# Where the streamed matmul operands start within 512 bytes of the on-chip memory

## The chip, the cores and the metric

The kernel runs on one core of a Trainium2 chip. The metric is device time in microseconds (us) of that core, from one execution of the whole program. Before the change it is 384.46 us, the median of 3 runs (384.4 to 384.72).

## The reference, cut to what matters

The input `x` has 8 sequences of 512 tokens with 128 features. Three blocks follow one another, each on a layer-normalised `x`, each added to `x`:

```
h = silu(x @ w1.T * s1) * (x @ w2.T * s2)     # 128 -> 512 (layers "0" and "1" of the code)
h = gelu(h @ h1.T * s)                        # 512 -> 512
h = gelu(h @ h2.T * s)                        # 512 -> 512
y = h @ w3.T * s3                             # 512 -> 128
x = x + 0.5 * y                               # then a recurrence, then the same again
```

The middle block is a recurrence over the 512 tokens, `h = tanh(x_t B + h A^T)` with 16 states, whose states go through `C` and `W_out`. All arrays are float32. The weights `w1`, `w2`, `h1`, `h2`, `w3` hold only -1, 0 and 1, so one fast matmul form is exact in them, while the activations need two parts.

## The kernel before, in words

Features lie on the 128 partitions, tokens along the free dimension. The tokens are cut into 8 chunks of N = 512; the feed-forward block runs 16 times (`g` from 0 to 15: 8 chunks before the recurrence, 8 after it). Every product of a feed-forward layer is made by `split_mm` (line 270): for each 128x128 tile of weights there are two TensorE matmuls of 512 columns, one that streams the high part of the activations and one that streams the low part, both into the same PSUM bank. The operand that streams past the array (the moving one) is a slice of 2,048 bytes in each partition; the other is loaded beforehand by a weight load (LDWEIGHTS) of 128 columns, 512 bytes in each partition. The rows write a matmul's inputs as moving, loaded: `y_hi,w_hi`.

The high parts are written as float32r (`xn_hi` by ScalarE at line 1190, `y1_hi` by ScalarE or VectorE, `y2_hi` and `y3_hi` by ScalarE at line 1216); the low parts are differences that VectorE (lines 802, 837) and GpSimd (lines 1489, 1495) write. In the text, layer 1 is the pair `w1`, `w2`, which streams `xn_hi` and `xn_lo`; layer 2 streams `y1_hi`, `y1_lo`; layer 3 `y2_hi`, `y2_lo`; layer 4 `y3_hi`, `y3_lo`.

The order of the work is written out by hand for each engine. A turn of TensorE (`early_turn`, `middle_turn`, `turn`) runs layer 2 of chunk `g`, layer 4 of `g - 1` within it, then layer 1 of `g + 1` between pieces of layer 3 of `g`. Between groups of 4 to 16 such streams stand short matmuls: transposes (4 of 128 columns at a time, line 282, 292 or 302, which stream `ident`), single steps of the recurrence (32 columns, line 437, which stream `h` against `a_mix`), and the products with `b_rep` and `cw_mix`. Engines wait for each other by semaphores; none of these waits depends on addresses.

What matters here is where tiles lie. `sb()` (line 61) reserves them one behind the other in the order of the calls. The small tiles and `gap` (line 105) end at byte 18,432 of each partition, which is 36 times 512. From there every tile is a multiple of 512 bytes: `w_raw`, `w_hi`, `w_lo`, and behind them all activations. So each weight tile that is loaded and each slice that is streamed begins at a multiple of 512 bytes. `WOFF` (line 72) and the sizes of the tiles make this so.

Of the kernel before, what the change touches and what calls it, by code (L numbers as in the profile page):

```python
# [21 lines left out]
F32R = mybir.dt.float32r  # L22
# [5 lines left out]
P = 128  # L28
# [12 lines left out]
N = HALVES * HCOLS  # L41
# [17 lines left out]
def build(nc, xT, xtok, w1T, w2T, h1T, h2T, w3T, scales, Ablk, Brep, CTrep, WoutT, ident_d, mask_d, outT):  # L59
    with ExitStack() as ctx:  # L60
        def sb(name, shape, dt=F32):
            return ctx.enter_context(nc.sbuf_tensor(name, shape, dt))
# [51 lines left out]
        outb = sb("outb", [P, N])  # L114
        xnt_f = sb("xnt_f", [P, N])
        xnt_m = sb("xnt_m", [P, N])
        xn_hi = sb("xn_hi", [P, N], F32R)
        xn_lo = sb("xn_lo", [P, N], F32R)
        xn2 = sb("xn2", [P, N])
        xb_all = sb("xb_all", [P, CHUNKS * HCOLS])  # L120
        th = sb("th", [P, 2, N])
        u = sb("u", [P, 2, N])
        y1 = sb("y1", [P, KT, N])
        y23 = sb("y23", [P, KT, N])
        y1_hi = sb("y1_hi", [P, KT, N], F32R)
        y1_lo = sb("y1_lo", [P, KT, N], F32R)
        y2_hi = sb("y2_hi", [P, KT, N], F32R)
        y2_lo = sb("y2_lo", [P, KT, N], F32R)
        y3_hi = sb("y3_hi", [P, KT, N], F32R)
        y3_lo = sb("y3_lo", [P, KT, N], F32R)  # L130
        ident = sb("ident", [P, P])
# [1550 lines left out]
```

## Time and profile before

| | us |
|---|---|
| median of 3 runs | 384.46 |
| the profiled execution | 385.06 |
| its span, first to last instruction | 383.1 |
| TensorE busy | 376.4 (98%) |
| VectorE busy | 279.7 (73%) |
| ScalarE busy | 268.0 (70%) |
| GpSimd busy | 163.9 (43%) |

The span is what the trace covers; 2.0 us of the profiled execution lie around it. A busy time says how long the engine had something in hand. For TensorE that says little of its pace, since matmuls overlap: the next one starts while the last one drains. The pace is read from the distance between the starts of two matmuls. Weight loads have their own rows (PEld) and lie beside the matmuls. "ns of one" is the time that the trace gives to one instruction, its drain included.

### The profile page before, as it was taken

Reading aid. Unit: us, or ns where it says so; the run is one execution under the profiler, and the core shown is the slowest. Engines: PE = TensorE matmul, PEld = TensorE weight load, DVE = VectorE, ACT = ScalarE, POOL = GpSimd, SP = SyncE. Lnnn points to the kernel's source line nnn. Section 1 sums busy time; section 2 is a strip of 40 time slices with the busy share of each in tenths; the row PEclk is TensorE's granted clock in tenths of the full one; section 3 lists DMA queues with packets and bytes.
Section 4 is the critical chain, followed back from the end, with each engine's and each line's share of the span. In section 5 each row is a group of like instructions: output and inputs, shape, how many; then the busy total and the mean of one; then the engine's idle time right before and its main releaser. Section 6 shows DMA issues by size and latency. Waiting matters only on the chain.

```text
span 383.1 us, 6587 instructions
## 1 busy us (share of the span) xinstructions
PE 376.4 (98%) x1793; PEld 300.2 (78%) x1793; DVE 279.7 (73%) x724; ACT 268.0 (70%) x625; POOL 163.9 (43%) x156
## 2 busy tenths in 40 slices
PE   8999999999999999999999999999999999999995
PEld 6777777778878787878778788888888888887774
DVE  4878989896777677576868866776767677686713
ACT  3889595777858688576784767758576775757654
POOL 3555262655525355142551633525334352533421
PEclk9999999999999999999999999999999999999999
DMA  7920000000000000000001001010100101000001
GB/s 226 436 110 1 27 2 27 3 2 28 2 28 0 2 27 0 28 2 28 27 2 56 2 8 49 0 55 2 41 14 0 55 0 55 0 30 26 2 28 32
DMA packets 6365, 14.00 MB, mean 37 GB/s; under 512 B 1088, under 2 KB 2112, under 8 KB 6080
## 3 DMA queue, kind: packets, MB, share of 16 engines
q1 hardware_dynamic: 5328, 13.37, 9.1%
q10 hardware_dynamic: 1008, 0.29, 0.3%
q8 instruction: 12, 0.20, 0.2%
q14 instruction: 17, 0.14, 0.1%
HBM read 7.37 MB, written 2.10 MB: 25 GB/s over the span
## 4 chain that ended last, share of the span: by engine, by line
PE 85%; issue 7%; POOL 3%; ACT 3%; DVE 2%; POOLq 0%; DVEq 0%
PE F L274 66%; PE FR L274 7%; PE SC L491 2%; PE FR L302 2%; POOL y_lo L1489 1%; PE SC L422 1%; POOL y_lo L1495 1%; PE F L519 1%; ACT y_hi L1216 1%; PE FR L292 1%; PE SC L274 1%; PE MI L302 1%; ACT y L1213 1%; PE F L521 1%; PE MI L282 1%
## 5 line engine op out<-in xcount | busy, mean ns | idle before, releaser
L274 PE MATMUL F<-y_hi,w_hi 128*128 128x512 f32 (+1 forms) x484 | 196.6, 407 | 0.3 <-DVE y_lo L1045 0.2
L274 PE MATMUL F<-y_lo,w_hi 128*128 128x512 f32 (+1 forms) x484 | 188.6, 390 | 0.0
L274 PEld LDWEIGHTS F<-y_hi,w_hi 128*128 128x128 f32 x484 | 90.9, 188 | 20.7 <-issue 2.2
L1213 ACT ACTIVATE y<-F,sc 128x512 f32<-128x512 f32 x111 | 76.1, 686 | 41.3 <-PE F L274 40.1
L274 PEld LDWEIGHTS F<-y_lo,w_hi 128*128 128x128 f32 x484 | 91.2, 188 | 15.9
L837 DVE TENSOR_TENSOR y_lo<-y,y_hi 128x512 fp32r<-128x512 f32 x79 | 64.8, 821 | 39.2 <-ACT y_hi L1216 39.2
L1489 POOL TENSOR_TENSOR y_lo<-y,y_hi 128x512 fp32r<-128x512 f32 x48 | 66.7, 1398 | 59.1 <-DVE y_hi L824 48.5
L1495 POOL TENSOR_TENSOR y_lo<-y,y_hi 128x512 fp32r<-128x512 f32 x48 | 62.6, 1310 | 34.6 <-ACT y_hi L1216 34.4
L1216 ACT ACTIVATE y_hi<-F,sc 128x512 fp32r<-128x512 f32 x111 | 76.1, 685 | 0.0
L1232 ACT ACTIVATE h<-SC 128x32 fp32r<-128x32 f32 x96 | 18.8, 196 | 48.0 <-PE SC L437 46.8
L274 PE MATMUL F<-xn_hi,w_hi 128*128 128x512 f32 x118 | 49.5, 419 | 0.1
L807 DVE SCALAR_TENSOR_TENSOR u<-th,F 128x512 f32<-128x512 f32 x61 | 41.5, 681 | 7.0 <-ACT th L1195 7.0
L274 PE MATMUL F<-xn_lo,w_hi 128*128 128x512 f32 x118 | 46.3, 393 | 0.0
L1481 POOL TENSOR_TENSOR ve_f<-mv_f,epsc 128x4 f32<-128x4 f32 x16 | 3.2, 202 | 96.6 <-DVE mv_f L768 91.6
L817 DVE SCALAR_TENSOR_TENSOR y<-F,s12h,u 128x512 f32<-128x512 f32 x58 | 43.3, 747 | 1.6
L1195 ACT ACTIVATE th<-F,s1h 128x512 f32<-128x512 f32 x61 | 41.1, 689 | 3.2 <-PE F L274 2.4
L856 DVE TENSOR_TENSOR h<-SC,h 64x32 fp32r<-64x32 f32 x96 | 17.1, 178 | 19.0 <-ACT SC L1233 18.2
L274 PEld LDWEIGHTS F<-xn_hi,w_hi 128*128 128x128 f32 x118 | 22.1, 187 | 6.9 <-DVE y L817 1.3
L274 PEld LDWEIGHTS F<-xn_lo,w_hi 128*128 128x128 f32 x118 | 22.2, 189 | 3.4
L274 PE MATMUL FR<-y_hi,w_hi 128*128 128x512 f32 x60 | 24.0, 399 | 0.0
L274 PE MATMUL FR<-y_lo,w_hi 128*128 128x512 f32 x60 | 23.4, 390 | 0.0
L437 PEld LDWEIGHTS SC<-h,a_mix 128*128 128x128 f32 x95 | 17.8, 188 | 6.6 <-DVE h L856 2.9
(170 smaller groups left out, 439.6 us busy)
## 6 DMA issues: line engine op xcount, KB each, us to landing
x_all<-in_xT SPq DMA_DIRECT2D x1, 2048.0 KB, 16.1
x_all<-x1c SPq DMA_DIRECT2D x8, 256.0 KB, 2.3
x_all<-lnin SPq DMA_DIRECT2D x8, 256.0 KB, 2.2
out<-outb SPq DMA_DIRECT2D x7, 256.0 KB, 2.0
x_all<-in_xtok SPq DMA_DIRECT2D x1, 1536.0 KB, 12.0
w_raw<-in_h1T SPq DMA_DIRECT2D x2, 512.0 KB, 7.8
w_raw<-in_h2T SPq DMA_DIRECT2D x2, 512.0 KB, 9.3
x_all<-in_xtok SPq DMA_DIRECT2D x2, 128.0 KB, 3.2
```

The lines of the kernel that those rows point to most:

```text
L274: mm = nc.tensor.matmul(out, wtile(w, layer, k, m), y, start=first and i == 0, stop=last and i == len(pairs) - 1)
L437: nc.tensor.matmul(SC[:, span(t)], a_mix[:, :], states, start=False, stop=True, skip_group_check=True).then_inc(step_mm, 1)
L807: nc.vector.scalar_tensor_tensor(out=u[:, m % 2, :], in0=th[:, m % 2, :], scalar=1.0, in1=l1_banks(g, m, late)[0][:, :], op0=ALU.add, op1= ...
L817: nc.vector.scalar_tensor_tensor(out=y1[:, m, :], in0=l1_banks(g, m, late)[1][:, :], scalar=s12h[:, m:m + 1], in1=u[:, m % 2, :], op0=ALU. ...
L837: nc.vector.tensor_tensor(y_lo[:, k, :], y[:, k, :], y_hi[:, k, :].bitcast(F32), ALU.subtract).then_inc(out_sem, 1)
L856: nc.vector.tensor_tensor(h[0:64, span(t)], SC[0:64, span(CSTEPS + t)], h[0:64, span(t)].bitcast(F32), ALU.subtract).then_inc(step_h, 1)
L1195: nc.scalar.activation(th[:, m % 2, :], l1_banks(g, m, late)[0][:, :], ACT.Tanh, scale=s1h[:, m:m + 1]).then_inc(th_r, 1)
L1213: nc.scalar.activation(y23[:, m, :], bankt[:, :], ACT.Gelu, scale=s)
L1216: nc.scalar.activation(y_hi[:, m, :], bankt[:, :], ACT.Gelu, scale=s).then_inc(hi_r, 1)
L1232: nc.scalar.activation(h[:, span(t)], SC[:, span(t)], ACT.Tanh)
L1489: pool.tensor_tensor(y1_lo[:, m, :], y1[:, m, :], y1_hi[:, m, :].bitcast(F32), ALU.subtract).then_inc(y1_lo_r if m < KT - 1 else y1_lo_las ...
L1495: pool.tensor_tensor(y_lo[:, k, :], y[:, k, :], y_hi[:, k, :].bitcast(F32), ALU.subtract).then_inc(out_sem, 1)
```

## The change

Four pads are added, and `xn_hi` and `xn_lo` are reserved later. Nothing reads or writes the pads. No instruction, order, semaphore or loop is changed; only addresses are.

```diff
-        xn_hi = sb("xn_hi", [P, N], F32R)
-        xn_lo = sb("xn_lo", [P, N], F32R)
         xn2 = sb("xn2", [P, N])
         xb_all = sb("xb_all", [P, CHUNKS * HCOLS])
         th = sb("th", [P, 2, N])
         u = sb("u", [P, 2, N])
         y1 = sb("y1", [P, KT, N])
         y23 = sb("y23", [P, KT, N])
+        past_x = sb("past_x", [P, 64])
+        xn_hi = sb("xn_hi", [P, N], F32R)
+        xn_lo = sb("xn_lo", [P, N], F32R)
+        past_1 = sb("past_1", [P, 80])
         y1_hi = sb("y1_hi", [P, KT, N], F32R)
         y1_lo = sb("y1_lo", [P, KT, N], F32R)
+        past_2 = sb("past_2", [P, 16])
         y2_hi = sb("y2_hi", [P, KT, N], F32R)
         y2_lo = sb("y2_lo", [P, KT, N], F32R)
+        past_3 = sb("past_3", [P, 80])
         y3_hi = sb("y3_hi", [P, KT, N], F32R)
         y3_lo = sb("y3_lo", [P, KT, N], F32R)
         ident = sb("ident", [P, P])
```

A pad of 64 floats is 256 bytes, one of 80 is 320, one of 16 is 64. Summed up and taken within 512, the streamed parts then begin 256 bytes (layer 1), 64 (layer 2), 128 (layer 3) and 448 (layer 4) past a multiple of 512. The weights stay where they were. `xn2`, `xb_all`, `th`, `u`, `y1` and `y23` lie 4,096 bytes lower and still at multiples of 512. The tiles behind the last pad (`ident`, `a_raw`, `a_mix`, `ct`, `wout`, `cw_rep`, `cw_mix`, the parts, `h`) lie 960 bytes higher, so 448 past a multiple of 512.

## Rows read from the trace of the kernel before

**Rows 1.** The page's busy times, and its line of the granted clock.
```profile
PE 376.4 (98%) x1793; PEld 300.2 (78%) x1793; DVE 279.7 (73%) x724; ACT 268.0 (70%) x625; POOL 163.9 (43%) x156
...
PEclk9999999999999999999999999999999999999999
```
**Rows 2.** Busy times by stretch: engines, then granted clock, DMA share, GB/s.
```profile
60.00:175.00 115.00, 114.92 (x580) 91.49 (x578) 86.28 (x242) 85.17 (x216) 52.60 (x51) 1.00 0.03 12
175.00:220.00 45.00, 45.00 (x230) 35.04 (x228) 36.39 (x102) 29.92 (x73) 18.56 (x19) 1.00 0.06 24
220.00:350.00 130.00, 130.00 (x614) 105.98 (x614) 93.43 (x234) 90.43 (x229) 53.86 (x47) 1.00 0.06 25
```
**Rows 3.** The chain that ended last, by engine.
```profile
PE 85%; issue 7%; POOL 3%; ACT 3%; DVE 2%; POOLq 0%; DVEq 0%
```
**Rows 4.** TensorE's groups by form: count, busy us, mean ns of one.
```profile
L274 PE MATMUL F<-y_hi,w_hi 128*128 128x512 f32 x476 | 194.4, 408 | 0.1
L274 PE MATMUL F<-y_lo,w_hi 128*128 128x512 f32 x476 | 186.6, 392 | 0.0
L274 PE MATMUL F<-xn_hi,w_hi 128*128 128x512 f32 x118 | 49.5, 419 | 0.1
L274 PE MATMUL F<-xn_lo,w_hi 128*128 128x512 f32 x118 | 46.3, 393 | 0.0
L274 PE MATMUL FR<-y_hi,w_hi 128*128 128x512 f32 x60 | 24.0, 399 | 0.0
L274 PE MATMUL FR<-y_lo,w_hi 128*128 128x512 f32 x60 | 23.4, 390 | 0.0
L302 PE MATMUL FR<-ident,xnt_f 128*128 128x128 f32 x60 | 9.6, 283 | 0.0
...
L274 PE MATMUL F<-xn_lo,w_lo 128*128 128x512 f32 x3 | 1.2, 389 | 0.0
```
**Rows 5.** Matmuls in order of time, late in a run of streams: start, duration.
```profile
127.16 0.39 PE L274 MATMUL F<-y_lo,w_hi 128*128 128x512 f32 x1
...
128.52 0.39 PE L274 MATMUL F<-y_lo,w_hi 128*128 128x512 f32 x1
```
**Rows 6.** Matmuls in order of time, behind four transposes.
```profile
180.56 0.60 PE L292 MATMUL FR<-ident,lnin 128*128 128x128 f32 x4
180.91 0.48 PE L274 MATMUL F<-y_hi,w_hi 128*128 128x512 f32 x1
181.22 0.40 PE L274 MATMUL F<-y_lo,w_hi 128*128 128x512 f32 x1
...
181.69 0.40 PE L274 MATMUL F<-y_lo,w_hi 128*128 128x512 f32 x1
181.93 0.39 PE L274 MATMUL F<-y_hi,w_hi 128*128 128x512 f32 x1
182.15 0.39 PE L274 MATMUL F<-y_lo,w_hi 128*128 128x512 f32 x1
...
183.08 0.40 PE L274 MATMUL F<-y_lo,w_hi 128*128 128x512 f32 x1
```
**Rows 7.** Weight loads in the stretch of Rows 5, then their group by form.
```profile
127.17 0.19 PEld L274 LDWEIGHTS F<-y_hi,w_hi 128*128 128x128 f32 x1
...
L274 PEld LDWEIGHTS F<-y_lo,w_hi 128*128 128x128 f32 x484 | 91.2, 188 | 15.9
```
**Rows 8.** A stream with no weight load beside it, all engines.
```profile
215.02 0.40 PE L274 MATMUL F<-y_lo,w_hi 128*128 128x512 f32 x1
215.35 0.16 PEld L422 LDWEIGHTS SC<-xn,b_rep 128*32 128x32 f32 x8 [0.37 <-ACT xn L1228]
```
**Rows 9.** The page's groups that write low parts, with idle time before.
```profile
L837 DVE TENSOR_TENSOR y_lo<-y,y_hi 128x512 fp32r<-128x512 f32 x79 | 64.8, 821 | 39.2 <-ACT y_hi L1216 39.2
L1489 POOL TENSOR_TENSOR y_lo<-y,y_hi 128x512 fp32r<-128x512 f32 x48 | 66.7, 1398 | 59.1 <-DVE y_hi L824 48.5
L1495 POOL TENSOR_TENSOR y_lo<-y,y_hi 128x512 fp32r<-128x512 f32 x48 | 62.6, 1310 | 34.6 <-ACT y_hi L1216 34.4
```

## The prediction

> **What bounds the kernel now.** I read the busy times first. TensorE has something in hand for 98% of the span, and the granted clock is full in every slice, which is its level of 2.4 GHz [rows 1]. By stretch the picture is sharper: from 60 to 350 us TensorE is busy 289.92 of 290 us, while VectorE has 216.1 and ScalarE 205.5 [rows 2]. The chain that ended last lies on TensorE for 85% and on issue for 7% [rows 3]. So time is set by how closely TensorE's matmuls follow one another, and not by how long another engine takes.
>
> Most of them are streams of 512 columns. The six groups of high and low parts in [rows 4] hold 2 x (476 + 118 + 60) = 1,308. Their busy times overlap, so I take the pace from starts. Late in a run of streams, six intervals take 128.52 - 127.16 = 1.36 us, or 226.7 ns each [rows 5]. I call this the settled pace; a stream there is given 0.39 us. Behind four transposes it is another: the first stream takes 181.22 - 180.91 = 0.31 us to the next, and the eight intervals after it take 183.08 - 181.22 = 1.86 us, or 232.5 ns each, single ones lasting 0.22 and 0.24 [rows 6]. The instruction is the same, its width is the same, no engine is waited for. At 2.4 GHz, 512 columns alone take 213.3 ns. So there are two losses: 13.4 ns in each settled stream, and another 6 ns or so in the unsettled ones.
>
> What differs between the two stretches? Not the weight tile: both walk through tiles that lie 512 bytes and more apart, and all streams begin at multiples of 512. Bits of the address above 512 therefore do not look like the cause. What is left is the phase in which one read falls against another, and the start within 512 bytes, which is the same everywhere in this trace. The next weight load starts within 0.01 us of its stream (127.17 against 127.16) and takes 188 ns of the 227 [rows 5, 7]. Two reads of the same memory then run side by side, one of 2,048 bytes and one of 512, both from the start of a 512-byte block. That is the one thing the change touches.
>
> **The change part by part.** *Instructions.* It adds and removes none: no DMA, no wait, no semaphore. A pad costs nothing at run time. What follows is all about the duration of instructions that stay.
>
> *The streams.* The trace has no stream at another offset, so I bound the effect from rows. The groups of low parts are the clean ones, because they never stand behind a short matmul. Their means are 392, 393 and 390 ns [rows 4] against 389 for a settled stream (the 0.39 of [rows 5], to the nanosecond in the small group at 389 of [rows 4]). The excess is 476 x 3 + 118 x 4 + 60 x 1 = 1,960 ns, 2.0 us. The high parts run in the same stretches, alternating with them, so they carry the same 2.0 us, besides the 0.09 us (0.48 against 0.39, [rows 6]) that each first one behind a short matmul loses because its successor's weights can only then be loaded. That last loss is one of order, and I leave it. If the shift lets the two reads fall in without colliding, all streams run at the settled pace: 4.0 us less. By the same measure the mean pace now is 226.7 + 3 = 229.7 ns.
>
> Beyond that the settled pace itself may move, since it is 13.4 ns above the 213.3 of the array. Bounds by rows: at the shortest single interval, 0.22 us, the streams would give 1,308 x 9.7 ns = 12.7 us; at 213.3 ns, 1,308 x 16.4 = 21.5 us. On the other side, at the unsettled 232.5 ns throughout they would cost 1,308 x 2.8 = 3.7 us; at the longest single interval, 0.24 us, 13.5 us, which no stretch of the trace holds for long. I take the 4.0 us, and 1.5 us for the settled pace (an estimate: about a tenth of its 13.4 ns, 1.2 ns on 1,308 streams). A whole removal is not likely, because a stream with no weight load beside it (the next load only 0.33 us after its start) is still given 0.40 us and not less [rows 8]; ends of matmuls are modelled, so this speaks only softly. Sum: -5.5 us.
>
> *The short matmuls.* `ident`, `a_mix`, `cw_mix` and `h` move by 448 within 512. Four transposes and their hand-over take 180.91 - 180.56 = 0.35 us [rows 6]. Were each transpose to change by 3 ns as the streams do, the 60 of the largest group [rows 4] would move 0.2 us, with either sign. The steps of the recurrence are 32 columns each, a sixteenth of a stream. I take nothing for both.
>
> *The other engines.* VectorE and GpSimd write the low parts to shifted places, at 821, 1,398 and 1,310 ns of one, and both groups sit idle before it for 39.2, 59.1 and 34.6 us in all [rows 9]. With starts still at multiples of 64 bytes I take nothing. Their cover is that idle time: an extra 1% on GpSimd's 129 us is 1.3 us and is swallowed by it. Where that cover is thin, in the 3% of the chain that lies on GpSimd [rows 3], 1% would cost 0.1 us. If TensorE becomes quicker by 5.5 us over 16 chunks, that is 0.34 us per chunk; VectorE, with 216 us of work in 290, does not become the bound [rows 2], but single waits on it and on ScalarE will eat some tenths of a microsecond, which I count into the range.
>
> **From span to time.** The profiled execution took 385.06 us with a span of 383.1. Less 5.5 it is 379.6. The median of the runs lies 0.6 lower than the profiled one, so I forecast 379.0 us.
>
> **The rivals.**
>
> *It changes nothing.* If the two reads have ports of their own, the start within 512 bytes can't matter and the unsettled pace has its cause within TensorE, for instance in how weights and streams are handed over. For it: the soft sign of [rows 8], where a stream alone isn't shorter, and that transposes, whose operands begin at multiples of 512 as well, run without a visible loss. Against it: the pace wanders between 0.22 and 0.24 us with nothing else to make it do so [rows 6]. It gives 384.5 us. The Trainium skill states this rule: "SBUF — State Buffer", section "Who interferes with whom", gives TensorE two independent read ports, one for the moving operand and one for weight loads, and says that it never waits on anyone. By that rule the change would be worth zero. The same skill's "TensorE: Matmul & The Clock Gate", section "Back-to-back issue gap", gives N/2.4 + 2.5 ns, an estimate of 215.8 ns for 512 columns; the trace does not agree, it has 226.7 at best over a run. So something costs these streams more than the pages tell, and that is why I give their rule less than half.
>
> *It is slower.* The order of short matmuls and streams stays, and with it the times at which runs of streams begin. With other offsets a run may never fall into the settled pace: then the streams of [rows 5] behave like those of [rows 6]. Place: every run longer than ten streams, above all layer 2 and 3. Price: 232.5 instead of 229.7 ns on 1,308 streams, +3.7 us, 388.2 us. It decides as soon as the mean pace exceeds 229.7. For it: the mean pace now, 229.7, lies midway between the settled 226.7 and the unsettled 232.5, so the pace that a random phase gives is about the present mean or worse. Against it: settling is what the streams do by themselves when left alone, so a phase without collisions exists and draws them in; it would be odd if only the offset 0 had one.
>
> *It is much faster.* The 13.4 ns of the settled pace are a collision too, of two reads that begin on the same 512-byte boundary at the same time, and the shift takes them away. At 1 to 2 ns above the array, about 215 ns, the streams save 1,308 x 14.7 = 19.2 us and the time is 365.3. For it: the loss is in every stream, as the equal starts are. Against it: [rows 8].
>
> **How the numbers follow.** Chances: forecast (the pace falls to between 220 and 229 ns, 372 to 383.6 us) 0.56; nothing 0.18; slower 0.18; much faster 0.08. The likeliest case alone has a range of 374 to 382.5. For 8 in 10 I leave out the much faster case and the worse half of the slower one, and put the ends at 370 (just past the 0.22 us bound, which is 371.8) and 387.5. About 0.2% (0.8 us) is what a measurement of this kernel can tell from no change. The forecast and the much faster case make faster 0.64, nothing makes the same 0.17 (a small part of it falls to each side), slower is 0.19.
>
> **What would show it.** In the profile of the changed kernel: TensorE's counts stay 1,793 and 1,793. The mean of the low-part groups falls from 392 and 393 to 389 or less, the starts behind transposes lie 227 ns apart at once and not after ten streams; if the settled pace moves, 128.52 - 127.16 has its like with less than 1.36 us. Layers 1 to 4 have different offsets, so if offsets matter they should show different paces, while the first stream behind a short matmul keeps its 0.31 us. Wrong would be: low-part groups at 392 again (nothing), or at 394 and more (slower). If they fall and the time doesn't, waits on VectorE, ScalarE or GpSimd have taken the gain, and the idle time before TensorE's weight loads would have grown. If the time falls while the starts keep their distances, the gain is from the writers of the low parts, which I have put at nothing.

## The result and the profile after

The changed kernel takes 386.85 us (median of 4 runs, 386.15 to 386.94) against 384.46. The ratio is 1.0062, 95% interval 1.0047 to 1.0077: slower by 2.4 us, where 5.5 us less had been forecast.

The page of the changed kernel, the lines that answer to [rows 1] (engine, busy us, instructions; then the clock by slice):

```profile
span 384.9 us, 6587 instructions
...
PE 378.0 (98%) x1793; PEld 299.5 (78%) x1793; DVE 279.9 (73%) x724; ACT 267.8 (70%) x625; POOL 164.1 (43%) x156
...
PEclk9999999999999999999999999999999999999999
```

Same instructions, same clock, and VectorE, ScalarE and GpSimd as busy as before. TensorE's groups by form, answering to [rows 4]:

```profile
L278 PE MATMUL F<-y_hi,w_hi 128*128 128x512 f32 x476 | 195.3, 410 | 0.1
L278 PE MATMUL F<-y_lo,w_hi 128*128 128x512 f32 x476 | 187.5, 394 | 0.0
L278 PE MATMUL F<-xn_hi,w_hi 128*128 128x512 f32 x118 | 49.5, 419 | 0.1
L278 PE MATMUL F<-xn_lo,w_hi 128*128 128x512 f32 x118 | 46.4, 393 | 0.0
L278 PE MATMUL FR<-y_hi,w_hi 128*128 128x512 f32 x60 | 24.2, 403 | 0.0
L278 PE MATMUL FR<-y_lo,w_hi 128*128 128x512 f32 x60 | 23.6, 394 | 0.0
```

Layer 1 (`xn`) stays at 393. The group into bank FR, which is layer 3's second row of tiles, goes from 390 to 394, the large mixed group from 392 to 394. The stretch of [rows 5], the same eight streams of layer 3, in the changed kernel (start, duration):

```profile
127.10 0.39 PE L278 MATMUL F<-y_lo,w_hi 128*128 128x512 f32 x1
127.34 0.39 PE L278 MATMUL F<-y_hi,w_hi 128*128 128x512 f32 x1
...
128.50 0.39 PE L278 MATMUL F<-y_lo,w_hi 128*128 128x512 f32 x1
```

Six intervals now take 1.40 us, 233.3 ns each, where they took 226.7. And the stretch of [rows 6], layer 2 behind four transposes:

```profile
180.77 0.60 PE L296 MATMUL FR<-ident,lnin 128*128 128x128 f32 x4
181.12 0.48 PE L278 MATMUL F<-y_hi,w_hi 128*128 128x512 f32 x1
181.44 0.40 PE L278 MATMUL F<-y_lo,w_hi 128*128 128x512 f32 x1
...
183.28 0.40 PE L278 MATMUL F<-y_lo,w_hi 128*128 128x512 f32 x1
```

Its eight intervals take 1.84 us, 230 ns each, against 232.5. So the change did act on the unsettled streams, and it took the settled pace away.

To sum this up I matched every matmul with its place in the program. For each stream I took the distance from its start to the start of the matmul behind it, left out those of 245 ns and more, and averaged them by layer, from layer 2 of chunk 1 to the start of the last chunk's layer 3:

| streams of (their number before) | offset | before, ns | after, ns |
|---|---|---|---|
| layer 1 (189) | 256 | 230.0 | 231.2 |
| layer 2 (425) | 64 | 230.2 | 231.0 |
| layer 3 (393) | 128 | 229.3 | 232.6 |
| layer 4 (117) | 448 | 229.4 | 232.9 |

Together these are 1,124 distances of 229.8 ns on average before (258.25 us) and 1,123 of 231.8 ns after (260.27 us). 2.0 ns on each of 1,124 is 2.3 us. From the start of chunk 2 (its first layer 1 stream) to the start of the last chunk's layer 3 TensorE needs 320.26 us before and 322.23 after, +1.97: the distances left out, and the short matmuls, took a little less. The profiled spans differ by 1.8 us only, because the changed kernel reached chunk 2 0.5 us earlier. Its warm-up streams were over sooner. The first row is before, the second after:

```profile
1.47 7.48 PE L491 MATMUL SC<-y_lo 128*128 128x512 f32 x19 [1.47 <-DVE y_lo L1060]
1.47 5.93 PE L495 MATMUL SC<-y_lo 128*128 128x512 f32 x19 [1.47 <-DVE y_lo L1064]
```

In the kernel before, 13 of the distances within these 19 are 426 or 427 ns, which is 512 columns at the clock's lower level of 1.2 GHz; after, 5 are. In the nine kernels of the experiments below it is 5 to 12, with the warm-up's two tiles always at the same start, so this is when the clock rose in an execution and not the addresses.

### The profile page after: what moved, and what is told of

Read it like the earlier page. It is cut to its first block, busy times and chain, and to the rows that moved or that the text cites. A ratio compares the mean times of both kernels' runs of the same rounds, so it can differ in the third digit from the quotient of the medians.

```text
span 384.9 us, 6587 instructions
## 1 busy us (share of the span) xinstructions
PE 378.0 (98%) x1793; PEld 299.5 (78%) x1793; DVE 279.9 (73%) x724; ACT 267.8 (70%) x625; POOL 164.1 (43%) x156
## 4 chain that ended last, share of the span: by engine, by line
PE 83%; issue 7%; POOL 4%; ACT 3%; DVE 1%; DMA 1%; SPq 0%; POOLq 0%; DVEq 0%
PE F L278 66%; PE FR L278 7%; PE FR L306 2%; POOL y_lo L1493 1%; DMA w_raw<-in_w2T 1%; PE F L523 1%; PE SC L426 1%; POOL y_lo L1499 1%; PE FR L296 1%; ACT y_hi L1220 1%; PE SC L278 1%; ACT y L1217 1%; PE MI L306 1%; PE F L525 1%; PE MI L286 1%
## 5 line engine op out<-in xcount | busy, mean ns | idle before, releaser
L1493 POOL TENSOR_TENSOR y_lo<-y,y_hi 128x512 fp32r<-128x512 f32 x48 | 66.8, 1395 | 59.8 <-DVE y_hi L828 48.5
L1499 POOL TENSOR_TENSOR y_lo<-y,y_hi 128x512 fp32r<-128x512 f32 x48 | 62.9, 1315 | 34.8 <-ACT y_hi L1220 34.6
```

The source lines that it names most:

```text
L1493: pool.tensor_tensor(y1_lo[:, m, :], y1[:, m, :], y1_hi[:, m, :].bitcast(F32), ALU.subtract).then_inc(y1_lo_r if m < KT - 1 else y1_lo_las ...
L1499: pool.tensor_tensor(y_lo[:, k, :], y[:, k, :], y_hi[:, k, :].bitcast(F32), ALU.subtract).then_inc(out_sem, 1)
```

## The experiments

Three theories at the start. A: the *distance* between the start of the stream and the start of the loaded tile, taken within some power of two, sets the pace a run of streams settles to, and 0 happens to be good. B: the stream's own start decides. C: neither; the writers of the shifted tiles disturb TensorE.

### The pace by itself: sweep

A program with nothing but streams: 32 of them per case, both operands at chosen starts.

```diff
+        for (name, _, wat), s in zip(CASES, streamed):        # 21 cases
+            w = weights[wat]
+            matmul(banks[3][:, 0:32], w[:, 0:P], s[:, 0:32])  # one short matmul ahead of each run
+            for i in range(32):
+                matmul(bank, w[:, i // 2 % 4 * P:][:, 0:P], s[:, i % 2 * N:][:, 0:N])
```

> A program of its own that leaves the whole reference computation out: 32 streams of 512 columns (float32r, all zeros) for each start of the streamed tile, 0 to 480 bytes past a multiple of 512 in steps of 32, the loaded tile at 0; then both tiles moved alike (64, 128, 448), then the loaded tile alone at 128 and 448. Theory A (the distance between the two starts within 512 bytes sets the pace that a run settles to): offset 0 settles to 226.7 ns, 64 near 229, 128 near 232 to 233, 448 above 229, 256 near 227; both moved alike gives 226.7 each time; the loaded tile alone at 448 gives what the stream at 64 gives. Theory B (the stream's own start decides, whatever the load does): both moved by 64, 128, 448 repeat the paces of the streams at 64, 128, 448, and moving the loaded tile alone gives 226.7. Theory C (start has no part, the slower paces of the changed kernel come from the writers of the tiles, since here no engine writes while TensorE runs): 226.7 for every case.

Rows of the sweep, one short matmul and its run of 32 streams per case (`zero` is stream and load at 0; the `s_` names say the stream's start; `both_` moves load and stream alike; `w_` moves the load alone):

```profile
34.49 0.18 PE L68 MATMUL B<-zero,weights 128*128 128x32 f32 x1
34.52 7.55 PE L72 MATMUL B<-zero,weights 128*128 128x512 f32 x32
...
49.51 7.58 PE L72 MATMUL B<-s_sixtyfour,weights 128*128 128x512 f32 x32
...
64.54 7.68 PE L72 MATMUL B<-s_onetwoeight,weights 128*128 128x512 f32 x32
...
72.08 7.74 PE L72 MATMUL B<-s_onesixty,weights 128*128 128x512 f32 x32
...
94.83 7.51 PE L72 MATMUL B<-s_twofivesix,weights 128*128 128x512 f32 x32
...
139.97 7.71 PE L72 MATMUL B<-s_fourfoureight,weights 128*128 128x512 f32 x32
...
155.12 7.51 PE L72 MATMUL B<-both_sixtyfour,weights 128*128 128x512 f32 x32
...
177.31 7.68 PE L72 MATMUL B<-w_onetwoeight,weights 128*128 128x512 f32 x32
184.86 7.57 PE L72 MATMUL B<-w_fourfoureight,weights 128*128 128x512 f32 x32
```

The settled pace, as the mean of the 16th to the 30th start-to-start distance of each run. Where a run repeats in a cycle that doesn't divide 15, another 15 give up to 0.7 ns more or less:

| stream past load, bytes | 0, 256 | 32, 288 | 64, 320 | 96, 352 | 128, 384 | 160, 416 | 192, 448 | 224, 480 |
|---|---|---|---|---|---|---|---|---|
| ns | 226.67 | 233.5 | 228.9 | 233.3 | 232.4 | 234.3 | 233.3 | 233.2 |

Each pair of distances that differ by 256 bytes agrees within 0.1 ns. Both moved alike by 64, 128 and 448: 226.67 each time. The load alone at 128 (distance 384): 232.3; at 448 (distance 64): 228.9. No other engine writes in this stretch, so C falls as the cause of this; B falls with the `both_` cases. Here the distance within 256 bytes decides. A settled run isn't always even: at 0 its distances repeat as 226, 227, 227; at 128 as 228, 230, 233, 241, 232, 231, 232; each distance has a cycle of its own, and these cycles are there in the changed kernel's layers 2, 3 and 4.

### Both operands moved in the kernel

```diff
-        gap = sb("gap", [P, 136])
+        gap = sb("gap", [P, 152])
```
with the four pads of the change left out, so that weights, streams and all else behind `gap` start 64 bytes past a multiple of 512.

> Weights and streamed parts both start 64 bytes past a multiple of 512 (the pad ahead of the weights is 64 bytes longer, the four pads of the change are gone, xn_hi and xn_lo keep their later place). Theory A (distance decides): paces of before, 226.7 settled, 384.5 us within 0.3. Theory B (the stream's own start decides): all layers settle to 229 and wander near 231, about +1.5 us, 386 us.

384.44 us against 384.25, ratio 1.0000, interval 0.9987 to 1.0013. Its layer 2 takes 230.05 ns, and chunk 2 to the last layer 3 is 0.07 us shorter than before. So the absolute start, moved by 64 bytes, has no part in the kernel either, nor has the later place of `xn_hi` and `xn_lo`. This run also says what a mean by layer is worth: its layer 1 takes 230.6 ns (before: 230.0) and its layer 4 228.8 (229.4) with every distance as before. Differences of 0.6 ns in layers 1 and 4, which have the fewest streams, carry no meaning; layers 2 and 3 differ by 0.1.

### One layer at a time

```diff
-        past_1 = sb("past_1", [P, 80])
+        past_1 = sb("past_1", [P, 16])        # layer 2 alone: past_x, past_2 left out,
+        past_2 = sb("past_2", [P, 112])       # the next pad closes the 512 again
```
and likewise for each of the others.

> Only layer 1's streamed parts start 256 bytes past a multiple of 512. The sweep has the paces repeat every 256 bytes, so 256 is 0. Theory A (distance within 256 bytes): paces as before, 384.3 us within 0.3. Theory of a period of 512 bytes (256 is the far end): layer 1 slower by 2 to 6 ns on its 256 streams, +0.5 to +1.5 us.

> Only layer 2's streamed parts start 64 bytes past a multiple of 512. Theory A or B: its streams take about 231 ns against 230.15 before, +0.2 to +0.6 us. Theory C: no difference from before.

> Only layer 3's streamed parts start 128 bytes past a multiple of 512; layers 1, 2, 4 and all tiles behind them at multiples. In the changed kernel layer 3's streams took 232.6 ns on average against 229.3 before. Theory A or B (start sets the pace): layer 3 near 232.5, the other layers as before but for the phase they are entered with, +1.0 to +1.6 us, most of the change's +2.4. Theory C (writers or the new order of the tiles): all layers alike, and the time moves with none of the layers in particular.

> Only layer 4's streamed parts start 448 bytes past a multiple of 512, which settled at 233.3 ns in the sweep. Theory A: its 128 streams take about 233 ns against 229.4, +0.4 to +0.5 us, and the layer 2 streams behind them start unsettled, +0.1. If the four layers' costs add up (about 0 + 0.7 + 1.0 + 0.5 us), no other part of the change is needed for its +2.4.

| alone | ratio, 95% interval | its streams, ns | chunk 2 to last layer 3, us |
|---|---|---|---|
| layer 1 at 256 | 0.9999, 0.9989 to 1.0009 | 230.0 to 230.1 | +0.02 |
| layer 2 at 64 | 1.0018, 1.0007 to 1.0030 | 230.2 to 230.6 | +0.64 |
| layer 3 at 128 | 1.0022, 1.0010 to 1.0033 | 229.3 to 232.3 | +0.91 |
| layer 4 at 448 | 1.0022, 1.0008 to 1.0036 | 229.4 to 232.8 | +0.58 |

The four ratios sum to +0.61%, the change is +0.62%; each of them has an interval of about 0.1% to either side, so their sum is known to some 0.25%. The stretch gives the same picture: +2.15 us in sum against +1.97, and the two kernels whose distances are as before within 256 bytes (layer 1 alone, both operands moved) lie within 0.1 us of the kernel before. In the kernel with layer 3 alone the group into FR, which holds only layer 3, goes from 390 to 394, while layer 1's doesn't rise (the same form as in [rows 4]); with layer 2 or layer 4 alone FR stays at 391:

```profile
L276 PE MATMUL F<-xn_lo,w_hi 128*128 128x512 f32 x118 | 46.3, 392 | 0.0
...
L276 PE MATMUL FR<-y_lo,w_hi 128*128 128x512 f32 x60 | 23.6, 394 | 0.0
```

Layer 1 at 256 costs nothing, as a period of 256 bytes says. The 1.2 ns that layer 1 lost in the changed kernel then come from something else, likely from its neighbours: with layer 4 alone moved it takes 230.8. Layer 2 costs more than its own streams do: of its 0.64 us only 0.2 are its own (425 x 0.46 ns); in its run layer 4 goes from 229.4 to 231.2, another 0.2 us, which is well above what traces differ by. Layer 3 rises by 0.4 ns; the 0.5 ns of layer 1 are within what traces differ by. My reading, which no run shows by itself, is that a run that is at another point of its cycle hands that on to the next layer.

### A uniform bad distance

```diff
-        past_x = sb("past_x", [P, 64])
+        past_x = sb("past_x", [P, 40])
-        past_1 = sb("past_1", [P, 80])
-        past_2 = sb("past_2", [P, 16])
-        past_3 = sb("past_3", [P, 80])
+        past_4 = sb("past_4", [P, 88])
```

> The streamed parts of all four layers start 160 bytes past a multiple of 512, the distance whose settled pace was the slowest of the multiples of 32 in the sweep, 234.3 ns; the tiles behind them at multiples of 512. Theory (the settled pace of the distance sets the time): the mean pace goes from 229.7 to about 234.3 ns, and 1,250 streams that follow a stream give +5.7 us, 1.5% slower, near 390 us. If the time depends only on how often runs enter unsettled, or on layers being at different offsets from each other, it stays near 384.5 to 386.

387.86 us, ratio 1.0099, interval 1.0084 to 1.0115. The mean pace came out at 233.9 ns, near the 234.3 of the sweep, and 4.1 ns more on 1,124 streams are 4.6 us. But chunk 2 to the last layer 3 grows by 3.4 us only. One stream before had waited, with 473 ns to the next start; that wait is gone (336 ns). The short matmuls take 0.6 us less, 0.4 of it at the steps of the recurrence, and there the idle time of TensorE's weight loads that VectorE's `h` ended goes from 2.9 to 2.5 us, that ended by its `y` from 1.3 to 0.9. So the mechanism was as expected, and of my +5.7 us, 1.1 were too high a pace and too many streams; the rest is in part that a slower TensorE waits less for VectorE. The three groups of low parts:

```profile
L276 PE MATMUL F<-y_lo,w_hi 128*128 128x512 f32 x476 | 188.4, 396 | 0.0
L276 PE MATMUL F<-xn_lo,w_hi 128*128 128x512 f32 x118 | 46.6, 395 | 0.0
...
L276 PE MATMUL FR<-y_lo,w_hi 128*128 128x512 f32 x60 | 23.7, 395 | 0.0
```

### Is anything better than 0, and what is the floor?

The second sweep takes finer starts, narrower loads, shorter streams, and bfloat16. Its loop is the first one's, with the number of loaded and streamed columns and the type as further parameters of a case.

> The reference computation is left out. 32 streams per case again, the loaded tile at 0. (1) Streams at 4, 8, 12, 16, 24, 40, 48, 80, 240 and 252 bytes. Theory A, distance within 256 bytes counted in lines of 16 bytes or so: 4 to 12 repeat 0 (226.7 ns), 16 and 240 are new values between 226 and 235; if one is under 226.7, a faster kernel follows. Theory A', distance counted in 64-byte blocks: 4 to 24 lie between the 226.7 of 0 and the 233.5 of 32, growing with distance. (2) Loads of 96, 64 and 32 columns beside the same streams at 0, and of 64 and 32 at 128. If the losses are two reads that meet, the loss falls with the length of the load: 226.7 falls towards 216 at 32 columns, and the 232.4 at 128 falls more. If the 13.4 ns over 213.3 is a fixed cost of a float32r stream, 226.7 stays for every load at 0. (3) Streams of 384 columns (160 ns at full clock): meeting reads leave the same 13 ns and 19 ns as with 512; a cost per column leaves 10 and 14. (4) bfloat16 for both operands, half the bytes: meeting reads need less of the memory, about 216 at every start; a fixed phase effect would show the same spread between 0, 32 and 128.

```profile
39.01 7.81 PE L76 MATMUL B<-s_four,weights 128*128 128x512 f32 x32
...
54.21 7.61 PE L76 MATMUL B<-s_twelve,weights 128*128 128x512 f32 x32
...
129.46 7.57 PE L76 MATMUL B<-loads_thirtytwo,weights 128*32 128x512 f32 x32
...
151.72 5.79 PE L76 MATMUL B<-short_zero,weights 128*128 128x384 f32 x32
157.38 5.88 PE L76 MATMUL B<-short_onetwoeight,weights 128*128 128x384 f32 x32
...
177.00 7.07 PE L76 MATMUL B<-half_onetwoeight,weights_half 128*128 128x512 bf16 x32
```

Settled paces in ns: 4 bytes 236.7, 8 bytes 231.4, 12 bytes 230.1, 16 bytes 231.5, 24 bytes 235.3, 40 bytes 234.5, 48 bytes 233.3, 80 bytes 231.1, 240 bytes 233.3, 252 bytes 230.2. None of the 17 starts tried within 256 bytes is under the 226.67 of distance 0, and 4 bytes, one float32 column, is the worst of all; 252 bytes, one column to the other side, is not. Both theories of lines and of blocks fall; the pace jumps from one column to the next.

Two reads that meet, as I had it in the prediction, is not shown to be the cause. At distance 0 a load of 96, 64 or 32 columns instead of 128 gives 230.1, 230.7 and 231.7 ns: the shorter load loses the good pace, and the loss grows instead of falling. At 128 it does fall, from 232.4 to 229.3 with 64 columns and 231.3 with 32, but not in step with the load. Streams of 384 columns settle at 173.3 ns at distance 0, which is 160 + 13.3, as 226.67 is 213.3 + 13.3: at these two lengths that part is per matmul, not per column. At 128 they take 176.0 ns, so the distance costs 2.7 ns there and 5.7 with 512 columns, which fits neither of the two figures expected. bfloat16 takes 215.8 ns at 0, 32 and 128 alike (2.5 ns over 213.3): at these starts no effect at all. So the loss belongs to float32r streams, has one part that is the same in each matmul, and another that depends on where stream and load start relative to each other. Why that is so stays open.

### The short matmuls between the runs

> The reference computation is left out. Runs of 16 streams, all at distance 0 and so settled at 226.7 ns at their end, each behind one matmul of 32 columns whose loaded and moving tiles start at 0, 64, 128, 448 or 256 past a multiple of 512, together or one alone; each case three times. If the short matmul's addresses set the entering phase, the number of unsettled streams behind it (10 behind the short matmul at 0 and 0) differs by case and is the same in all three of a case. If not, all thirty runs are alike.

Rows of that program, the short matmul with both operands at 0, with both at 64, and with its loaded tile alone at 448 (start; a case ends where the next begins):

```profile
22.43 0.18 PE L67 MATMUL B<-plain,load_plain 128*128 128x32 f32 x1
...
26.21 0.18 PE L67 MATMUL B<-plain,load_plain 128*128 128x32 f32 x1
...
33.75 0.18 PE L67 MATMUL B<-both_sixtyfour,load_both_sixtyfour 128*128 128x32 f32 x1
...
37.51 0.18 PE L67 MATMUL B<-both_sixtyfour,load_both_sixtyfour 128*128 128x32 f32 x1
...
75.20 0.18 PE L67 MATMUL B<-load_fourfoureight,load_load_fourfoureight 128*128 128x32 f32 x1
...
78.98 0.18 PE L67 MATMUL B<-load_fourfoureight,load_load_fourfoureight 128*128 128x32 f32 x1
```

To the nanosecond these are 3.786, 3.754 and 3.780 us for the same 17 matmuls. Behind the short matmul at 0, at 256, or with its stream alone moved, the run's distances are 321, 233, 236, 224, 231, 236, 228, 233, 231 and then 226.7; behind both at 64 or both at 448: 317, 232, 231 and then 226.7; behind both at 128: 316, 236, 228, 232, 231. With the loaded tile alone moved the long stretch stays: at 448 it is 312, 229, 234, 235, 225, 230, 236, 229, 232, 231, and at 128 it is 318 and then as at 0. Each case is the same all three times within 1 ns. So the unsettled stretch of [rows 6] looks like a fixed path: its distances, to the nanosecond, hold the same 233, 236, 224, 231, 236, 228, 233 in a row. Where a run enters that path depends on the short matmul's two starts together: moving its stream alone changed nothing, moving its load alone changed the entry but cut nothing, and moving both alike cut the path to two to four distances. Three kernels tried to use it:

```diff
+        past_4 = sb("past_4", [P, 16])        # 112 in the first kernel
         ident = sb("ident", [P, P])           # in the third the pad stands ahead of a_mix
```

> All streamed parts at multiples of 512, only the tiles behind them (ident, a_mix, cw_mix, h and the rest) 448 past one. In the changed kernel the first streams behind a short matmul took 316 ns against 318. Theory: the short matmuls' addresses set the phase in which the next run of streams begins, so the time moves by up to 0.5 us either way, and all layers alike; rival: these addresses have no part, 384.3 us within 0.2.

> Streams at multiples of 512, all tiles behind them 64 bytes past one. Behind a short matmul with both its tiles at 64 runs settled after 2 streams instead of 9 (entry run), worth 32 ns each if they were entered settled. Most runs of the kernel are 8 streams long and so are entered unsettled; theory: a gain of 0.3 to 1.0 us, layer 3 and 2 quickest. Rival: the order of phases in the kernel washes it out, within 0.2 us of before.

> As the one before, but ident and a_raw stay at multiples of 512, so only the recurrence's tiles (a_mix, cw_mix, h) and those between move by 64 bytes. If the gain of the moved tail comes from the 95 recurrence steps, this has all of it; if it comes from the transposes' ident, none.

Ratios 0.9996 (0.9986 to 1.0005), 0.9992 (0.9981 to 1.0003) and 0.9988 (0.9977 to 1.0000). In the traces, chunk 2 to the last layer 3 is 0.40, 0.28 and 0.59 us shorter than before, and kernels with unchanged distances differed from it by under 0.1 us. All three point the same way, but even the lowest ratio, 383.79 us against 384.12, is at the edge of its interval. I call it a likely 0.1%, not a shown one. The third kernel moves the recurrence's tiles without `ident` and isn't behind the second, so nothing here speaks for the transposes; the differences are too small to say more.

## Why the prediction was wrong

- **The bound was right.** TensorE's start-to-start distances set the time. The mean pace went from 229.8 (229.7 in the prediction) to 231.8 ns, and the time followed: 2.3 us by the streams, 2.4 measured. Nothing of size is left over for another engine.
- **The step that failed** is "if the shift lets the two reads fall in without colliding, all streams run at the settled pace". I had read the settled 226.7 ns as what streams do "by themselves when left alone", a floor that the offset 0 kept them from for ten streams, and argued that "it would be odd if only the offset 0 had one". It is odd, and so: of 0 and the 17 starts tried within 256 bytes, only 0 settles at 226.7. Layers 2, 3 and 4 went to distances that settle at 228.9, 232.4 and 233.3. Layer 1, at 256, has the same 226.7 in the sweep, and gained nothing. The unsettled streams at 0, at 232.5 ns, were the price of entry to the best pace. The 4.0 us of that term have the wrong sign: -4.0 forecast, +2.3 measured in the streams.
- **The further 1.5 us for the settled pace** failed with it. The 13.3 ns over 213.3 were the same with both operands moved alike by 64, 128 and 448 and stayed with shorter streams; no distance went below them.
- **What I had no right to conclude.** The trace of before holds one offset. From it I inferred that bits of the address above 512 have no part, which fits (the period is even 256), but the direction needed a second offset, and I gave one side 0.64. The 386.85 us do lie within my 370 to 387.5, but in the part of it that belonged to the slower rival; the likeliest case had ended at 382.5.
- **The rival "slower"** was the one that came true, in its direction and nearly in size: +3.7 us at 232.5 ns was its price, +2.4 at 231.8 the result. Its place was right too, layers 2 and 3; layer 4 came with them. Its mechanism was half right: a run does never "fall into the settled pace" of 226.7, but not because it stays unsettled. In the sweep runs at 64, 128 and 192 (which is 448 within 256) settle within a few streams, in slower cycles of their own.
- **The rival "it changes nothing"** rested on the Trainium skill, "SBUF — State Buffer", section "Who interferes with whom", by which TensorE's two read ports are independent. What I took from it, that the start can't matter, does not hold where float32r is streamed: moving the load alone by 128 bytes changes the pace from 226.7 to 232.3 ns. Whether the ports are what couples the two, no run shows. For bfloat16 nothing speaks against it, with 215.8 ns at each of three starts. The Trainium skill's "TensorE: Matmul & The Clock Gate", section "Back-to-back issue gap", gives N/2.4 + 2.5 ns for the gap of a single matmul, which is 215.8 for 512 columns. The bfloat16 runs, each stream with a weight load of its own, agree with that figure; the same section's figure of about 131 ns for a steady stream of loads and matmuls of 512 columns is met by no run here, of which the fastest has these 215.8.
- **At nothing, rightly:** the writers on VectorE and GpSimd (814, 1,395 and 1,315 ns of one against 821, 1,398 and 1,310), and, as far as can be told, the short matmuls: with the tail alone moved by the same 448 bytes the stretch is 0.40 us shorter in one trace, and the ratio, 0.9996, is not clear of 1.

## What to carry to other kernels

Where float32r matmuls of 512 columns follow one another, start each streamed tile and each loaded tile at the same place modulo 256 bytes; here every other distance tried cost 2 to 10 ns per matmul, and in this kernel the four layers at 160 cost 1.0% of its time. bfloat16 showed no such effect at the three starts tried. And before reading a steady pace in a trace as a floor that everything tends to, vary the thing it may depend on in a small program of its own: one of 200 us gave 21 cases and would have settled the sign of this change.

## What was not expected of the hardware

- Start-to-start distances of float32r streams depend on the distance of stream and load within 256 bytes, from 226.67 ns (0) to 236.7 ns (4 bytes), in cycles that repeat to the nanosecond.
- A run entered behind a short matmul follows a fixed path of 3 to 10 unsettled distances (the first one included), and how much of it depends on where that short matmul's loaded and streamed tile start.
- At distance 0 the same 13.3 ns over 512 / 2.4 and 384 / 2.4 stand in a float32r matmul of 512 columns (226.67) and of 384 (173.3); in bfloat16 it is 2.5 ns with 512 (215.8).
